# A graph network on one core: ScalarE issues the loads of the pair tables' blocks, empty places move to the front of the first turn, steps ask for their sums one turn later, zero rows in runs of 1280 bytes

## The reference

```python
x = layernorm(x + L0(x))   # wx = x@W.T+b; wx * segment_sum(w**2 * wx[dst] by src), self loops out
x = layernorm(x + L1(x))   # agg = segment_sum(concat(x[src], edge_attr)@W1+b1, by dst); concat(x, agg)@W2+b2
x = layernorm(x + L2(x))   # two weighted mean aggregations with relu between
x = layernorm(x + L3(x))   # three rounds: t_k = h@W_et[k].T+b; a = segment_sum(t[etype][src], dst); h = GRU(a, h); then a gate
```

## Time and profile before

| what | us |
|---|---|
| three timed executions | 14902.51, 14829.66, 14875.42 |
| their median | 14875.42 |
| the profiled execution | 14825.95 |
| its span, from the first to the last instruction | 14824.3 |

### The profile page before, as it was taken

One profiled execution on the slowest core, in us unless ns is written; L12 is line 12 of the kernel. 1 busy time (PEld: TensorE's weight loads), 2 busy tenths in 40 slices (PEclk: granted clock), 3 DMA queues, 4 the chain that ended last, 5 costly groups with the idle time before them and its releaser, 6 DMA issues. The chain is left out here.

```text
span 14824.3 us, 166292 instructions
## 1 busy us (share of the span) xinstructions
PE 9912.4 (67%) x37230; PEld 6043.2 (41%) x37231; DVE 4854.0 (33%) x18913; ACT 1607.7 (11%) x4318; POOL 9042.1 (61%) x8448
## 2 busy tenths in 40 slices
PE   5777777886677665444445554788867888577775
PEld 3444443226545443333333333344433444344443
DVE  3333334552322222222233333233332333322224
ACT  1111112222100000000000000111100000000001
POOL 2888888770366565666656665666656666566662
PEclk6555556778777776666667777899988999788887
DMA  8999998998534332333334443666646666366663
GB/s 283 220 221 221 223 221 114 115 117 193 126 94 99 90 95 71 92 91 91 83 95 119 115 117 95 187 209 207 211 128 197 209 206 213 122 190 187 190 190 92
DMA packets 2883133, 2275.44 MB, mean 153 GB/s; under 512 B 1211014, under 2 KB 2655107, under 8 KB 2882796
## 3 DMA queue, kind: packets, MB, share of 16 engines
q1 hardware_dynamic: 2403570, 1628.59, 37.2%
q0 software_dynamic: 447568, 628.96, 22.0%
q10 hardware_dynamic: 31722, 15.04, 0.4%
HBM read 1545.67 MB, written 755.00 MB: 155 GB/s over the span
## 5 line engine op out<-in xcount | busy, mean ns | idle before, releaser
L1634 PE MATMUL bank<-work 128*128 128x512 f32 x4704 | 2312.7, 636 | 581.5 <-DMA work<-t_pairs 345.3
L1068 POOL DMA_INDIRECT ring<-t_types,stage x1728 | 1669.9, 966 | 1239.3 <-ACT stage L1253 727.9
L2136 DVE TENSOR_TENSOR acc<-acc,bank 128x128 f32 x1704 | 487.4, 286 | 5402.6 <-remote 3824.9
L1043 POOL DMA_INDIRECT t_sums<-ring,stage x1136 | 1763.1, 1552 | 455.5 <-issue 273.0
L1068 POOL DMA_INDIRECT ring<-t_x,stage x1152 | 1119.9, 972 | 1410.4 <-ACT stage L1253 1071.0
L1634 PEld LDWEIGHTS bank<-work 128*128 128x128 f32 x4704 | 910.2, 204 | 1579.0 <-issue 1124.1
L1653 PE MATMUL bank<-ring 128*128 128x128 f32 x6912 | 1123.2, 307 | 574.0 <-issue 418.0
L1653 PEld LDWEIGHTS bank<-ring 128*128 128x128 f32 x6912 | 1046.8, 220 | 922.9 <-issue 797.5
L1068 POOL DMA_INDIRECT more_rows<-t_types,stage x840 | 798.6, 951 | 373.4 <-issue 256.1
L2159 DVE TENSOR_SCALAR ring<-iota_f,meta_low 128x128 f32<-128x128 f32 x4544 | 1001.4, 292 | 0.1
L1514 PE MATMUL bank<-aux 128*128 128x128 f32 x2272 | 528.8, 408 | 572.7 <-ACT aux L1193 560.7
(11 more groups left out here) (319 smaller groups left out, 14712.1 us busy)
## 6 DMA issues: line engine op xcount, KB each, us to landing
work<-t_pairs SPq DMA_DIRECT2D x588, 1024.0 KB
t_pairs<-acc SPq DMA_DIRECT2D x544, 648.0 KB
work<-t_pairs SPq DMA_DIRECT2D x588, 256.0 KB
t_types<-work SPq DMA_DIRECT2D x216, 512.0 KB
work<-t_types SPq DMA_DIRECT2D x294, 256.0 KB
aux<-t_pairs SPq DMA_DIRECT2D x196, 256.0 KB
work<-t_x SPq DMA_DIRECT2D x108, 256.0 KB
ring<-t_types,stage POOLq DMA_INDIRECT x1728
```

The costliest lines, as they stand in the source:

```text
L1043: pool.indirect_dma_start(TAB[k], bass.IndirectOffsetOnAxis(ap=stage[:, u:u + 1], axis=0), msg[:, u, :], None, compute_op=ALU.add).then_in ...
L1068: pool.indirect_dma_start(gathered[par][u], None, table, bass.IndirectOffsetOnAxis(ap=stage[:, par * U + u:par * U + u + 1], axis=0)).then ...
L1634: mm = pe.matmul(o, dense_t[:, tile, k_ * D:(k_ + 1) * D], dense_b[:, half, :, k_ * HALF:(k_ + 1) * HALF], start=first and k_ == 0, stop=e ...
L2136: v.tensor_tensor(into, into, bank[q][:, 0:P], ALU.add).then_inc(added, 1)
```

## The change

- `unit_rows` leaves SyncE. ScalarE gets `block_rows`, the same two transfers, called behind the stage copy of places 1 to 3 of each turn (ahead of the step's part there). In passes 4 to 6 the first two blocks go ahead of all stage copies. In passes 1 to 3 a tile's rows of the node table now go with its second half.
- PAD = 3 empty places: they are numbered first, in turn 0, and every engine skips them and increments its semaphores by 3 instead. SURE becomes 71, so no turn of these inputs is in the tail.
- `done_by` and the plan of groups (`need`) go by 2*NQ + 1 in place of NQ + 1 and by 2*NQ - PAD in place of NQ.
- ZEROS = 280 for each table, ZA = 1280.
- SyncE doesn't wait for a pass's stores at its end any more; the first load of the next layer pass does, and ScalarE did already.

```diff
-SURE = ((NGR - HG) // NQ - 1) | 1
+PAD = -(NGR - HG) % NQ
+SURE = (NGR - HG + PAD) // NQ
+STEPS = LEAD + 1
+FIRST_PLAIN = 2 * (LEAD + 2)
 ZEROS = (SURE - 1) * NQ
-ZA = -(-PAIR_LEN // (ZEROS * P * 4)) * 4
+ZA = -(-PAIR_LEN // (ZEROS * P * 64)) * 64
+        def places_of(t):
+            return range(PAD if isinstance(t, int) and t == 0 else 0, NQ)
+        def uses(t, q):
+            return t if q < PAD else t + 1
...
-            return ph * ADDS if tail_ else m * (2 * NQ) + ((ph - 1) * ADDS + NQ + 1)
+            return ph * ADDS if tail_ else m * (2 * NQ) + ((ph - 1) * ADDS + 2 * NQ + 1)
...
-            def unit_rows(ph, table, p, c):
...
             def scatter(t):
-                for q in range(NQ):
+                for q in places_of(t):
                     go(staged, nth(t, q))
...
                 with turns(pool, 0, SURE // 2) as p:
-                    turn(p * 2, 0)
+                    turn(p * 2, 0, places=range(PAD, NQ))
                     turn(p * 2 + 1, 1)
-                turn(SURE - 1, 0)
+                    turn(p * 2 + 2, 0, places=range(PAD))
+                turn(SURE - 1, 0, places=range(PAD, NQ))
...
+                def block_rows(p, c):
+                    half, tile = c % NH, c // NH
+                    unit = p * (NH * TILES) + ((ph - 1) * UNITS + c)
+                    at = bass.ds((p * TILES + tile) * P, P)
+                    if ph > 3:
+                        wait(act, dense_done, unit - 1)
+                        act.dma_start(dense_b[:, half, :, :], PAIR_BLOCKS[half][at, :, 0:KT * HALF]).then_inc(dense_in[c], 16)
+                    else:
+                        field = (F_ONE if ph == 1 else F_W) * HALF
+                        wait(act, dense_done, unit + (1 - NH * TILES) if not isinstance(p, int) else max(unit + (1 - NH * TILES), (ph - 1) * UNITS))
+                        act.dma_start(dense_w[:, c, :, :], PAIR_BLOCKS[half][at, :, field:field + HALF]).then_inc(dense_in[c], 16)
+                    if half == int(ph < 4):
+                        act.dma_start(dense_t[:, tile, :] if ph > 3 else dense_x[:, tile, :], table[at, :]
+                                      ).then_inc(dense_x_in[tile], 16)
+                def turn(t, par, part=None, places=parts, block=None):
                     for q in range(NQ):
-                        wait(act, summed, (ph - 1) * PS + last(t, q) - NQ)
-                        at = par * U + q * K
-                        act.activation(stage[:, at:at + K], cols(index, t * U + q * K, K), ACT.Copy).then_inc(staged, 1)
+                        if q in places_of(t):
+                            wait(act, summed, (ph - 1) * PS + last(t, q) - NQ)
+                            at = par * U + q * K
+                            act.activation(stage[:, at:at + K], cols(index, t * U + q * K, K), ACT.Copy).then_inc(staged, 1)
+                        if block is not None and q:
+                            block(q - 1)
                         if part is not None and q in places:
                             part(q)
...
-            link(v.tensor_scalar(need, iota_f[:, 0:STEPS], float(2 * NQ), float(NQ), ALU.mult, ALU.add))
+            link(v.tensor_scalar(need, iota_f[:, 0:STEPS], float(2 * NQ), float(2 * NQ - PAD), ALU.mult, ALU.add))
```

More of the change, by code:

```diff
@@ L649, in _ @@
             used = used_turns(mybir.EngineType.SP)
+            scattered = loaded(mybir.EngineType.SP, turns_by[0:1, 3:5], 2, TURNS * 16, "sixteen for each turn")
             def zero_piece(table, at, n, parts):
@@ L744, in feature_rows, with features_in, stream_pass @@
                              S_ATTR[bass.ds(edge[q], GE), :].rearrange("(k p) f -> p k f", p=P)).then_inc(attr_in[q], 16)
-            def features_in(t, unit=None):
+            def features_in(t):
                 edge = slot_regs(mybir.EngineType.SP, edge_row, t, EP - GE)
-                for q in range(NQ):
+                for q in places_of(t):
                     feature_rows(t, q, edge)
-                    if unit is not None and q:
-                        unit(q - 1)
-            def stream_pass(ph, table, load, store, late=None):
+            def stream_pass(ph, load, store, late=None):
                 def body(p, units):
@@ L762, in body @@
                             store(p - 2)
[L764 to L773, removed]
                         if ph == 1:
[L775 to L778, removed]
+                            features_in(p * 2 + a)
                     if late is not None and not (isinstance(p, int) and p < 2):
                         late(p - 2)
-                if ph == 1:
-                    for i in range(TILES):
-                        unit_rows(ph, table, 0, i)
                 pairs_of_turns(sp, body)
@@ L1062, in gather, with turn @@
             def gather(ph, table):
-                def turn(t, par, *_):
-                    for q in range(NQ):
+                def turn(t, par, pair=None, places=range(NQ)):
+                    for q in places:
                         go(staged, ph * PS + nth(t, q))
@@ L1214, in _ @@
                     msg_keep(t, q - 1)
+            keeps(1)
+            with turns(act, 2, SURE) as t:
+                keeps(t)
             msg_keep(SURE - 1, NQ - 1)
@@ L1523, in _ @@
                 dup_sums(0, q)
-                if q:
+                if q > PAD:
                     messages(0, q - 1)
@@ L1618, in gather_pass @@
                 used = used_turns(mybir.EngineType.PE)
-                uses = loaded(pe.engine, turns_by[0:1, 0:2], 2, TURNS // 2 + 1, "half of the turns each")
-                landed = [used * 16 + uses[par] * (4 * 16 * (ph - 1)) + 4 * 16 for par in range(2)]
+                halves = loaded(pe.engine, turns_by[0:1, 0:3], 3, TURNS // 2 + 1, "half of the turns each")
+                scattered = loaded(pe.engine, turns_by[0:1, 3:4], 1, TURNS * 16, "sixteen for each turn")[0]
+                by_uses = [scattered + n * (K * 16 * (ph - 1)) for n in halves]
+                landed = [[by_uses[0 if q >= PAD else 2] + (K * 16 if q >= PAD else 0) for q in range(NQ)],
+                          [by_uses[1] + K * 16 for q in range(NQ)]]
                 def unit(p, c):
@@ L1673, in body @@
                         turn(p * 2 + 1, 1, p, lambda i: block(TILES + i), lambda q: late[q](p - 1, g), late)
+                wait(pe, summed, (ph - 1) * PS)
+                pe.sem_inc(summed, PAD)
                 pairs_of_turns(pe, body)
-                turn(SURE - 1, 0, SURE // 2)
+                for t in range(FIRST_PLAIN, SURE):
+                    turn(t, t % 2, t // 2)
                 def no_turn(t, n):
@@ L2152, in turn @@
                         off = nodes(t - 1)
-                    for q in range(NQ):
-                        if not first:
+                    for q in places_of(t):
+                        if not first and q in places_of(t - 1):
                             v.wait_ge(summed, (ph - 1) * PS + last(t, q))
@@ L2192, in gather_steps @@
                     link(v.tensor_tensor(into, into, bank[4 + i // NB][:, i % NB * HALF:(i % NB + 1) * HALF], ALU.add))
+                for t in range(FIRST_PLAIN + 1, SURE):
+                    turn(t)
                 def last_sums(t):
```

173 lines of the change are left out of this document (97 added, 76 removed).

## The result

The changed kernel took 14911.58 us (median of 8, 14893.23 to 14960.81) where the kernel before took 14867.84 on the same chip: ratio 1.0038, 95% interval 1.0022 to 1.0053. That is 44 us slower, where 1.1% faster was forecast. It lies inside the stated range, but with the wrong sign; the range, 14,380 to 14,930, was wide because it spanned rivals that work in opposite ways, and it is luck that the time falls inside it.

A forecast was written before the change was run, and what follows sets the result against it. GpSimd's scatter count bounds the scatter stage; the ring of gather, hot matrix, sum and stage paces the passes, 6.06 us per place. -20 - 72 + 0 + 0 - 40 = -132 from 14825.95: 14694, put at 14,705; range 14,380 to 14,930.

The forecast's parts named there:

- The move, -40: All six passes: ScalarE issuing the blocks in place of SyncE gives -40 us, between -500 and +300.
- 40 us regained from t_pairs: Passes 4 to 6: TensorE's wait for t_pairs, 345.3 us before, shrinks, giving -40 us.
- sign of being wrong: Passes: the prediction is wrong if the pace of 6.06 us per place changes, up or down; 0.1 us is 169.
- rival D: Passes 4 to 6: ScalarE becomes the bound through block waits (332 us) and issues (192); +430, 15,260; chance 0.14.
- once in eight: Ring with eight places: a delay of one stage copy is passed on only once in eight.
- The places, -72: Six passes: skipping three empty places saves 12 us per pass, -72 us, between 0 and -109.
- the conditional tail: Turns 69 and 70 leave the tested tail: 0, no more than a couple of us.
- Rival C: Heads of passes: turn 0's units hide the saved places, the move does nothing; -20 to +20, 14,840; chance 0.17.
- The scatter stage, -20: Scatter stage: GpSimd issues 12 scatters fewer, 22.3 us; net -20, between -22 and 0.
- +28 for more bytes: Scatter stage: zero rows write 6.0 MB more; 0 expected, +28 us if the DMA engines set the stage's end.
- Steps a turn later, 0: Steps wait for sums a turn later, a wait already met: 0, range 0 to +20 us.
- The crawls (B): Passes 1 to 3: SyncE's issue bursts cause the crawls, which go; up to -450 us, about 14,350; chance 0.22.

The follow-up runs named there:

- c1: The changed kernel plus a few bounds assertions, as control on a slow chip: 14912.76 us, 1.0039 of the kernel before.
- e1b: The changed kernel with blocks and table rows back on SyncE, on a slow chip: 14841.61 us, 0.9989 of the kernel before.
- e1: The changed kernel with blocks and table rows back on SyncE, on a fast chip: 12975.77 us, 0.9965 of the kernel before.
- e3: The changed kernel with VectorE's memset of the accumulator cut into 26, on a fast chip: 12944.04 us, 0.9942 of the kernel before.
- e9: The changed kernel with MID = SURE, one skipped stretch in place of three, on a slow chip: 14885.23 us, 1.0020 of the kernel before.
- e13: The changed kernel with blocks back on SyncE, MID = SURE and both memsets cut, on a fast chip: 12909.10 us, 0.9905 of the kernel before.
- c0: The changed kernel plus a few bounds assertions, as control on a fast chip: 12985.32 us, 0.9969 of the kernel before.
- b0: The kernel before, run again for one execution on a fast chip: 13021.62 us.
- e6: The kernel before with only the blocks moved to ScalarE, on a fast chip: 13036.75 us, 1.0006 of the kernel before.

## Why the prediction was wrong

The forecast was -132 us: -92 for places and scatters, -40 for the move. On the slow chip of c1 and e1b it came as -23 and +71.

- *The move, -40*: the step that failed with its sign. It was put together as +10 in passes 4 to 6 and -50 in 1 to 3. Measured on the slow kind, it is +71 (c1 against e1b); by the traces about +50 in passes 4 and 5 and some +30 in 1 to 3. In 4 to 6 the prediction set 40 us regained from t_pairs against 50 for later stage copies; TensorE's wait did fall, by 128 us, but ScalarE's lateness grew by 302. In 1 to 3 it held that with six buffers ScalarE's lateness costs nothing and that part of the crawls goes; no gain came. The prediction's own sign of being wrong was met: a place took 6.50 us of passes 1 to 5 (9136 us over 5 x 281, heads and ends included) for 6.36 before (9028 over 5 x 284), though in the middle of pass 6 it is 6.09 (319 gathers in 486 us) for 6.06. This is rival D at its place, and by its sign (GpSimd's wait for L1253 well above 640: 841), at about a seventh of the 524 us that its two terms had before the savings. Its "once in eight" is not refuted: 302 us of lateness against some 50 us is one in six.
- *The places, -72*: the term that was mis-sized, on both kinds. With the move taken out (e1, e1b) the whole gain is 49 and 23 us, of which the scatter stage has 36 to 40; the passes gained about nothing. What ate the 15 us per pass is in the main shown: the hold at the memset (41 us in e3) and VectorE's two further skips (28 in e9, with the uncertainty said there). The prediction looked at turn 0's units, and not at what else stands at the head and end of a pass: it held the conditional tail for "0, and no more than a couple of us", where it was some 28. Rival C had the size, places worth little, for another reason: turn 0's units don't hide them, as e13's passes show.
- *The scatter stage, -20*: measured -40 in the first pair of traces and -36 in c0 against b0. 22 are the 12 scatters. The other 14 to 18 are less waiting between scatters; no run settles why. The +28 for more bytes didn't come.
- *Steps a turn later, 0*: no run separates it; e13's gain leaves little room for a cost.
- *The crawls (B)*: stretches in which an engine's instructions stand apart for no reason that the profile shows. Moving the blocks off SyncE didn't shorten passes 1 to 3 (1897, 1736 and 1824 us after), and on the fast kind the same code runs without them. They go with the chip, not with SyncE's bursts. B's price doesn't add up either: three passes of 1,600 us are 619 under 5419, not 450.
- *The Trainium skill's rule* that initiating on several engines saves only the initiating ("DMA: Bandwidth & Descriptors", section "Issuing engines are not separate DMA queues") would have given 0 for the move. The runs on the fast kind agree (10 us in e1, 1.0006 in e6, neither told from none); the +71 us on the slow kind are no saving either, but a cost.

## What to carry to other kernels

A transfer moved to an engine brings its semaphore wait and its issue time along. On an engine of the loop that sets the pace that can cost more than it gives back elsewhere: here 71 us, the larger part where there were two buffers, and it seems not nothing with six. When work is dropped at the head or the end of a loop, look at what then stands next to what: here a long memset and a chain of skipped turns took back what twelve gathers gave. Measure on more than one chip where a latency chain sets the pace: the sign of this change differed between them.

## What was not expected of the hardware

- Chips differ by 14% on this program (13024 to 13034 against 14865 to 14909 us) with steady times on each. The difference is in the ring: 6.06 or 5.02 us a place. On the slow kind the crawl at the head of pass 4 in the trace before has single matmuls whose starts, from 9325.97 on, are 2.80, 2.11, 2.09, 2.80, 2.80, 2.10, 1.40 and 0.70 us apart, all near multiples of 0.70. In its six passes TensorE has some 260 steps of 0.70 or 1.40 us between two starts, and in those of b0 some 20. What sets this step is open.
- A gather of GpSimd held for up to 14.8 us (c1, pass 1) by a long memset of VectorE with hot matrices directly behind it; with an add or another memset behind, none was held.
- Runs of 1260 bytes in place of 1280 made the scatter stage 140 us longer.
